# A queue depth of two for GpSimd's indirect DMAs in a gated delta-rule attention with a routed FFN

## The reference

```python
def step(S, inp):                                   # 512 steps, one state S (8 x 8) per head
    k_t, q_t, v_t, beta_t, a_t = inp
    S = S * a_t[..., None, None]
    kv_mem = jnp.einsum('bhd,bhde->bhe', k_t, S)
    delta = (v_t - kv_mem) * beta_t
    S = S + k_t[..., :, None] * delta[..., None, :]
    y_t = jnp.einsum('bhd,bhde->bhe', q_t, S)
    return (S, y_t)
...
ctx = _rmsnorm(ys, norm_w) * jax.nn.silu(gate)
x = _layernorm(x + ctx @ Wo.T + bo)
...
routing_indices = jnp.argmax(x @ router_w.T, axis=-1)      # one of E = 8 experts for each token
for e in range(E):                                         # I = 352 inner channels
    mask = (routing_indices == e)[..., None]
    xe = jnp.where(mask, x, 0.0)
    ye = (jax.nn.silu(xe @ gate_w[e].T) * (xe @ up_w[e].T)) @ down_w[e].T
    out = out + jnp.where(mask, ye, 0.0)
x = _layernorm(x + out)
```

## Time and profile before

| | |
|---|---|
| three runs | 775.88, 781.50, 783.81 us, median 781.50 |
| the profiled execution | 779.52 us, of which the core's span is 777.7 |
| busy | PE 677.5 us (87%), POOL 654.0 (84%), DVE 610.1 (78%), ACT 415.8 (53%) |
| indirect DMAs to `x_sorted` (L344) | 64, POOL busy 62.7 us |
| indirect DMAs to `out` (L509) | 71, POOL busy 70.9 us |
| mean granted TensorE clock | 0.928 |

### The profile page before, as it was taken

One profiled execution on the slowest core, in us unless ns is written; L12 is line 12 of the kernel. 1 busy time (PEld: TensorE's weight loads), 2 busy tenths in 40 slices (PEclk: granted clock), 3 DMA queues, 4 the chain that ended last, 5 costly groups with the idle time before them and its releaser, 6 DMA issues.

```text
span 777.7 us, 13705 instructions
## 1 busy us (share of the span) xinstructions
PE 677.5 (87%) x3545; PEld 507.4 (65%) x3545; DVE 610.1 (78%) x1554; ACT 415.8 (53%) x1281; POOL 654.0 (84%) x800
## 2 busy tenths in 40 slices
PE   8779798989989899999989989697788879999990
PEld 3446374756657575565756657575667879999990
DVE  3899999999999999999999999999953523333340
ACT  6735456564565656466565555433314346666660
POOL 2899899999999999999999999999755756766664
PEclk9889899999999999999999999799869999999995
DMA  6733233443333334333234232206346456777720
GB/s 175 198 97 98 69 98 86 114 116 90 86 90 94 89 112 116 96 85 102 82 105 120 77 97 71 85 22 220 136 164 184 166 182 226 240 237 235 238 97 9
DMA packets 135917, 97.27 MB, mean 125 GB/s; under 512 B 95630, under 2 KB 110225, under 8 KB 135714
## 3 DMA queue, kind: packets, MB, share of 16 engines
q1 hardware_dynamic: 130514, 87.55, 38.2%
q0 software_dynamic: 4320, 8.43, 3.4%
q10 hardware_dynamic: 1008, 0.43, 0.2%
HBM read 39.80 MB, written 31.43 MB: 92 GB/s over the span
## 4 chain that ended last, share of the span: by engine, by line
DVE 35%; PE 29%; POOL 20%; issue 5%; ACT 5%; DMA 3%; SPq 2%; POOLq 0%; DVEq 0%; ACTq 0%
PE banks L432 11%; DVE banks L1817 6%; DVE upd L1805 6%; POOL q_prod L1255 6%; PE banks L654 5%; PE banks L445 5%; DVE banks L1791 5%; DVE prod L1775 4%; DVE banks L1801 4%; DVE mix L1795 3%; POOL u L1255 3%; DVE upd L1786 3%; POOL solve L1255 2%; POOL kkqk L1255 2%; POOL u_tmp L1255 1%
## 5 line engine op out<-in xcount | busy, mean ns | idle before, releaser
L1255 POOL TENSOR_TENSOR q_prod<-s_keep,q_gam 128x512 f32<-128x512 f32 x128 | 139.9, 1097 | 12.0 <-ACT s_keep L965 11.7
L707 PE MATMUL banks<-q_prod,ident 128*128 128x256 f32 x496 | 118.9, 395 | 21.6 <-POOL q_prod L1255 21.4
L965 ACT ACTIVATE s_keep<-banks 128x128 f32<-128x128 f32 x128 | 49.8, 389 | 156.7 <-DVE upd L1805 156.6
L707 PEld LDWEIGHTS banks<-q_prod,ident 128*128 128x128 f32 x496 | 95.7, 198 | 46.2 <-POOL q_prod L1255 32.4
L542 DVE TENSOR_TENSOR hid<-banks,silu 128x384 f32<-128x384 f32 x71 | 39.6, 557 | 96.4 <-PE banks L432 83.8
L432 PE MATMUL banks<-xs_t,w_tile 128*128 128x128 f32 x852 | 108.9, 278 | 3.5 <-ACT silu L473 3.5
L1817 DVE TENSOR_REDUCE banks<-upd 128x128 f32<-128x640 f32 x127 | 105.0, 827 | 7.6 <-ACT z_s L1194 0.5
L432 PEld LDWEIGHTS banks<-xs_t,w_tile 128*128 128x128 f32 x852 | 102.4, 194 | 4.4 <-issue 4.3
L1791 DVE TENSOR_REDUCE banks<-prod 128x64 f32<-128x576 f32 x128 | 93.7, 732 | 0.0
L654 PE MATMUL banks<-kkqk,ident 128*128 128x320 f32 (+2 forms) x272 | 84.5, 471 | 7.7 <-ACT y_rms L993 4.3
L1775 DVE TENSOR_TENSOR prod<-banks,k_gam 128x512 f32<-128x512 f32 x128 | 88.1, 688 | 2.9
(11 more groups left out here) (214 smaller groups left out, 1442.3 us busy)
## 6 DMA issues: line engine op xcount, KB each, us to landing
w_tile<-gate_up_we SPq DMA_DIRECT2D x71, 352.0 KB, 3.0
xs<-x_sorted SPq DMA_DIRECT2D x71, 64.5 KB, 2.4
x_ct<-in_x_ct SPq DMA_DIRECT2D x16, 256.0 KB, 3.2
k_dram<-kq_s SPq DMA_DIRECT2D x16, 256.0 KB, 2.9
q_dram<-kq_s SPq DMA_DIRECT2D x16, 256.0 KB, 3.6
out<-v_s SPq DMA_DIRECT2D x16, 256.0 KB, 2.7
out<-beta SPq DMA_DIRECT2D x16, 256.0 KB, 2.6
k_h<-k_dram SPq DMA_DIRECT2D x16, 256.0 KB, 3.0
```

The source lines that it names most:

```text
L707: i = mm(out, ident[:, :], q_prod[m][:, :, d, :], start=(m == 0 and d == 0), stop=(d == DH - 1), skip_group_check=True)
L1255: b.step(label, win, lambda: tt(out, x, y, op))
```

## The change

Each indirect DMA of POOL waits until the last but one of its kind has landed. For the sort, the semaphores `s_sorted_a` and `s_sorted` become two each, used in turn, since one semaphore shared by two DMAs in flight doesn't tell which has landed; DMA n of a part waits for DMA n - 2 of the same part. Tile 24 and tile 25, the first two of the second part, wait for none. SP waits for both semaphores where it waited for one. For the scatters, `scatter(tile)` waits for `scatter(tile - 2)` by the semaphores that are there already.

```diff
-        s_sorted_a, s_sorted = sem("s_sorted_a"), sem("s_sorted")
+        s_sorted_a, s_sorted = ([sem(f"s_sorted_{part}{n}") for n in range(2)] for part in "ab")
...
             for m in range(t0, t1):
+                part, n = (s_sorted_a, m) if m < WA * TW else (s_sorted, m - WA * TW)
+                if n >= 2:
+                    eng.wait_ge(part[n % 2], 16 * (n // 2))
                 eng.indirect_dma_start(t["x_sorted"], bass.IndirectOffsetOnAxis(ap=place[:, m:m + 1], axis=0),
-                                       x1_all[:, m, :], None).then_inc(s_sorted_a if m < WA * TW else s_sorted, 16)
+                                       x1_all[:, m, :], None).then_inc(part[n % 2], 16)
...
-            eng.wait_ge(s_sorted, 16 * (NT - WA * TW))
+            for n in range(2):
+                eng.wait_ge(s_sorted[n], 16 * len(range(n, NT - WA * TW, 2)))
...
             def scatter(tile):
                 after(eng, s_norm, tile)
+                after_scatter(eng, tile - 2)
                 eng.indirect_dma_start(t["out"],
...
-                e.wait_ge(s_sorted_a, 16 * WA * TW)
+                for n in range(2):
+                    e.wait_ge(s_sorted_a[n], 16 * WA * TW // 2)
```

## The result

| | before | after |
|---|---|---|
| median of the runs | 781.23 us (4) | 793.92 us (4) |
| lowest, highest | 775.88, 783.81 | 789.07, 795.64 |
| the profiled execution, its span | 779.52, 777.7 | 795.64, 793.8 |

The ratio is 1.0161 with a 95% interval of 1.009 to 1.0233: some 12.7 us slower, where 3.2 were forecast. The median lies 0.9 us above the range of the prediction. The two profiled executions lie 16.1 us apart, 3.4 more than the medians, so what their stretches differ by doesn't have to add up to 12.7.

What follows compares the result with a forecast made beforehand. PE was taken as busy throughout the expert tiles, POOL mattering only beyond its slack. Window 15's 1.4, the sort's end's 1.8 and the scatters' 0 gave 3.2 us on a 781.5 median: 784.7 us, range 779 to 793.

Steps and rivals of the forecast that it cites:

- Windows 4 to 14 and the ten DMAs from 572.6 on: Sort DMAs whose waits cost nothing: landed long before, or 2.9 us late and covered by 4.97 us of idle time.
- The time from a landing to the start: Every waiting indirect DMA starts 0.30 us after the landing, so a wait is free up to a 2.2 us landing.
- Window 15: Sort DMAs wait for landings of 6.4 and 6.6 us, delaying `ctx_t` by 1.4 us; bounds 0 and 4.6.
- no further delay: In window 15, the pair behind the late pair loses nothing more, as landings there take 3.3 us or less.
- The sort's end: Last 24 sort DMAs take 6.6 us more, 4.8 covered, so PE's gap grows by 1.8 us; bounds 0 and 5.2.
- The scatters: Expert stage: POOL falls 0.1 us behind per group, 0.6 in all, borne by slack; cost 0, bounds 0 and 4.1.
- The second rival: POOL bounds the scatters in groups of four, 645 to 684 us, at landings above 3.3 us; 792.2 us, chance 0.25.
- The end: Last scatters, on the path: with landings of 2.1 to 2.3 us the waits cost nothing.
- All hidden: Rival over the whole kernel: the last but one has landed anyhow, waits cost nothing; 781.5 us, chance 0.20.

Runs made afterwards that it cites:

- exchanged: Kernel before with landing waits in the scatters alone, written ahead of the norm's wait so that the DMA carries the landing's: 780.36 us, 0.9987.
- The light kernel: Changed kernel with copies of expert weights cut to a quarter of their columns from the seventh tile on: 785.45 us, 1.0050.
- the sort only: Changed kernel without the scatters' wait, so only the sort DMAs wait: 789.59 us, 1.0112 to the kernel before.

## Why the prediction was wrong, point by point

- **Windows 4 to 14 and the ten DMAs from 572.6 on: nothing.** Right. `ctx_t` of the last window still has 3.47 us of idle time ahead of it of the 4.97, and neither half of the sort loses there.
- **The time from a landing to the start: 0.30 us at most, taken once for all.** Half right. It is 0.27 where the landing's wait rides on the DMA and 0.77 where it is an instruction of its own. The listing in the section on the change shows two waits on each scatter, and the prediction didn't ask how an instruction holds two. It named "if a wait costs POOL more than 0.30 us" among what would make it wrong, and gave it no price in the scatters.
- **Window 15, +1.4 us.** Measured 2.3 us (0.9 to 3.6), inside the bounds, and 2.65 in the profile. The landing of the burst was 7.10 us for 6.6, which makes the delay 3.8 us for 3.3. The three idle times that were to absorb 1.93 are gone as reckoned, but the DMAs at 553.36 and 560.78 now have 0.56 and 0.45 us of idle time ahead of them for some 0.17. Each starts 0.77 us behind the landing it waits for (549.08 + 3.5 + 0.77 = 553.35): the "no further delay" behind the burst was reckoned with the 0.30.
- **The sort's end, +1.8 us.** This step failed: 5.9 us (3.8 to 8.0), 4.1 more than forecast and above its bound of 5.2. The slack was right: 4.8 us were to be hidden and 5.0 to 6.0 were. What failed is the term of 6.6 us for the 24 DMAs, which was 9.9 in the kernel after and 11.4 alone (9.2 to 12.9 in the four kernels with these waits). By the model above, most of that is the median standing for the landings (5.1), and the rest the form (1.5).
- **The scatters, 0.** This step failed by most: 4.6 us (2.3 to 6.9), and 0 in the other form. The landings were right, 2.3/2.7/4.7 in the kernel after for 2.3/2.8/4.0. With 2.8 the third of a group starts 3.57 us behind the first for the 3.1 taken, so a group of four falls behind by 3.57 - 2.63 - 0.37 = 0.57 us instead of 0.1, 3.4 over six of the 3.7 of slack, and the landings over 4 us pass it. The second rival had the mechanism, the place and the point of decision, and only put it at landings above 3.3 us. With 0.77 for 0.30 that point is 2.8, which is the median. Its time, 792.2, is the nearest to the measured 793.92, but it came from landings of 4.0 us and a bound for the sort, so that nearness is in part luck.
- **The end, nothing.** From PE's last product to POOL's last scatter it is 10.7 us for 9.7 before, in this and in the other kernel with the wait in front, and 9.7 when exchanged. So 1.0 us, from the form again: 2.3 + 0.77 is beyond 2.63.
- **All hidden (0.20).** Its condition was landings below about 2.9 us, which doesn't fit its own sum: 0.42 us a pair is a landing of 2.65 (2.65 + 0.30 - 2.53). The light kernel is below either with its median of 2.4 and hides the scatters and most of the sort's end. By the Trainium skill, "DMA: Bandwidth & Descriptors", section "Anatomy of one DMA — SWDGE (gpsimd) path", it would be 2.15 us for 66 KB, an estimate by that page. The minima of 2.3 bear it out, and the loaded landings, up to 7.1, don't.
- **A term that was missing: PE's clock.** After a gap the clock comes back late. These are the windows view's stretches of before (the gap ends at 637.88) and of after (at 646.33), and one of after where PE had waited 2.35 us for `xs_t`:

```profile
636.00:644.00 8.00, 6.12 (x40) 6.12 (x41) 1.41 (x3) 3.05 (x12) 2.83 (x3) 0.79 0.61 183
```

```profile
644.00:652.00 8.00, 5.67 (x27) 5.67 (x28) 0.85 (x2) 3.96 (x15) 5.14 (x5) 0.51 0.45 126
...
684.00:692.00 8.00, 5.65 (x41) 5.41 (x41) 1.60 (x4) 3.23 (x14) 3.94 (x5) 0.84 0.55 180
```

The granted clock is at its lower level (0.51 of full, 1.2 GHz) all through the 5.67 us that PE works up to 652, and falls again where PE waited. PE's first 100 instructions behind the gap take 12.8 us before, 13.9 after, 13.0 with the waits in the last 40 alone and 12.7 in the sort only. So the clock adds up to 1 us or so to what a longer gap costs. It doesn't go by the gap's length alone: with the waits in the scatters alone the 100 take 13.7 us behind a gap of 6.6.

In sum: 2.3 + 5.9 + 4.6 = 12.8 us for the 12.7 measured, where 1.4 + 1.8 + 0 stood. Two terms were wrong at the root: the 0.30 us from a landing to the start, which is 0.77 where the landing's wait stands in front, and the median of 2.8 us in place of the landings one by one. Window 15, the join and the slack there were as the prediction had them; the 1.0 us at the end, which is a part of the scatters' 4.6, it had at nothing.

## What to carry to other kernels

Reckon a chain of waits for landings by the landings one by one and through the order of issue. Their median leaves out that the mean lies above it, and what two coupled chains lose to each other, here together half of the cost (5.1 of 39.1 - 29.0 us). Where an instruction waits for two things, find out which of the two it carries itself, and let that be the one that comes last. One exchanged line was worth 4.6 us here. And with landings of 2.3 to 5 us and 1.26 us from issue to issue, a depth of three costs nothing measurable and a depth of two 1.6%.

## What the runs showed of the hardware

- From a landing to the start of the indirect DMA that waits for it: 0.27 us with the wait on the DMA, 0.77 us with it in front as an instruction of its own. They repeat to 0.01 us in the kernel after, in that with the waits in the scatters alone, in the exchanged one and in that with the waits in the last 40 alone.
- A wait that has been met costs POOL's issue nothing measurable: 0.9992 (0.9967 to 1.0018) with the same number of waits at depth four.
- Landings of 66 KB by an indirect DMA took 2.3 us at the least (the scatters' 2.1). The scatters' median goes with the DMA engines' load: 2.7 us at a DMA share of 0.64 and 2.4 at 0.37, with single landings of 4.7 and 4.2. Beside a transfer of 1.5 MB one of the sort took 7.1.
